# Layer normalisation on ScalarE, five decay buffers, two C-row buffers and a new order of steps

## The chip, the cores and the metric

The kernel runs on one core of a Trainium2 chip. The core has TensorE (PE: matmuls into PSUM banks), VectorE (DVE), ScalarE (ACT), GpSimd (POOL) and SyncE (SP), which here only issues DMA transfers. Each engine works through its own list of instructions in order; semaphores order them against each other. The metric is the device time of one execution in microseconds, lower is better.

## The reference, cut to what matters

Eight batches of 512 tokens with 128 features go one by one through two blocks.

```
xn = layernorm(x)                                  # (x - mean) / sqrt(var + 1e-5)
s  = attention(xn)                                 # own token masked out
g  = silu(sum over 8 experts of gate_e * expert_e(xn))   # top 2 of 8, computed densely
x  = x + s * g
xn = layernorm(x)
s  = mamba(xn)        # rmsnorm, in_proj, conv, selective scan over 512 tokens, out_proj, + xn
g  = silu(routed_expert_ffn(xn))                   # one of 8 experts per token
x  = x + s * g
```

The selective scan keeps, for 256 channels and 16 states, `s = s * dA + dBu` along the tokens, and sums `s * C` over the states.

## The kernel before, in words

**Groups of steps.** The work of a batch is cut into named steps in five groups. A: first layer norm (ln0, xn), transposes xT, gating (gl, gate), attention (q, k, v, s, p, o), dense experts (h0 to h15, m0 to m7, b2), silu. H: second layer norm (ln1, xm), mamba input (hT, xi, z, u, bc, bm, bl), routing (sc, rk, which gives each token its position), dl, ln and du (softplus, delta), put (POOL scatters the tokens to DRAM by position), fetch. S: the scan, with 32 scans i = 2n + h for state n and half of channels h; d is a decay on ACT (exp), b spreads a row of B with a matmul, scan is done by DVE (input times du, then the scan), p multiplies by the row of C on POOL, a adds the product into yacc with an identity matmul (h = 0) and e adds it on POOL (h = 1), c loads a row of C by DMA, spread over the partitions. F: routed expert FFN (w loads expert weights, ld and xs load and transpose tokens, h, y, st stores, get gathers, ft, silu). C: the end of a batch (y, op, xr, out). P: preparation of weights; P.pe (`beta_products`, L926 to L935) is 64 matmuls of one column with 128x128 weights, whose sums are needed by scaled_weights on DVE (dve 2).

**Order.** Five batches overlap: while S and F work on batch b, H is at b+1, A at b+2 and C at b-1 (`AHEAD`, L344). `ROWS` (L59) gives every step a place in a batch, in fractions of a batch, small shifts for ACT, DVE and POOL, and a PSUM bank; `OWN` (L324) gives other places for the first batches. `program` (L364) sorts them into a list for each engine. PE and SP follow the plain order of places. Nothing is decided at run time: an engine that waits holds all that stands behind it.

**The layer norms.** DVE computes mean and variance (`moments`, L1116 to L1122: four bn_stats, four bn_aggr), POOL computes rstd by a power (L1418, L1419; for the second norm also rstd2, L1425 to L1428), and DVE normalises four tiles of 128x128: xn at L1146 and xm at L1214. ACT scales the second by rstd2 (L1001). PE transposes the results (xT L718, x1T L761, hT L765).

**Around the scan.** The decays dA have four buffers (`DECAYS`, L41): decay s waits until scan s - 4 is done (L1083). The rows of C have three (`C_BUFS`, L42): SP may issue the load of row r when all products of row r - 3 are done (L659), and holds its other transfers meanwhile. rk is L786 to L790 on PE, its positions end with L1271 on DVE. gl is L722, q and k L725, v L728, s L736 and L737, p L743, o L752, expert h L823 and m L829, F.h L854, F.y L862 and L864, b L877, a L886 and L888, op L905, dl L800. All work of ACT is issued from L944.

Of the kernel before, what the change touches and what calls it, by code (L numbers as in the profile page):

```python
# [40 lines left out]
DECAYS = 4  # L41
C_BUFS = 3  # L42
# [10 lines left out]
def group_tiles(k):  # L53
# [371 lines left out]
def build(nc, ins, out, xs_dram, ys_dram, kept_dram, c_dram):  # L425
    nc.disable_value_cache = True
    ctx = ExitStack()
    with ctx:
# [151 lines left out]
        def state(s):  # L580

            n, h = divmod(s, NH)
            return st[:, STATES[h][n]]
# [973 lines left out]
```

## Time and profile before

| | us |
|---|---|
| median of 3 runs | 982.8 (982.41 to 982.96) |
| the profiled execution | 983.75 |
| its span | 981.9 |
| PE busy | 855.8 (87%) |
| DVE busy | 810.0 (82%) |
| ACT busy | 608.9 (62%) |
| POOL busy | 587.6 (60%) |
| mean granted clock of PE | 0.936 |

The shares are means over a head of some 150 us in which DVE and POOL have little to do, periods in which all five groups overlap, and a tail in which first A and then H are missing. Timeline rows give the start in us from the start of the span, the length in us, engine, line, operation and count; in brackets stands the idle time before, with what ended it. "busy" is the time in which an engine had something in work; latencies of instructions that follow each other can overlap a little. A granted clock of 1.00 is TensorE's 2.4 GHz, 0.50 is 1.2 GHz.

### The profile page before, as it was taken

Reading aid. Unit: us, or ns where it says so; the run is one execution under the profiler, and the core shown is the slowest. Engines: PE = TensorE matmul, PEld = TensorE weight load, DVE = VectorE, ACT = ScalarE, POOL = GpSimd, SP = SyncE. Lnnn points to the kernel's source line nnn. Section 1 sums busy time; section 2 is a strip of 40 time slices with the busy share of each in tenths; the row PEclk is TensorE's granted clock in tenths of the full one; section 3 lists DMA queues with packets and bytes.
Section 4 is the critical chain, followed back from the end, with each engine's and each line's share of the span. In section 5 each row is a group of like instructions: output and inputs, shape, how many; then the busy total and the mean of one; then the engine's idle time right before and its main releaser. Section 6 shows DMA issues by size and latency. Waiting matters only on the chain.

```text
span 981.9 us, 15767 instructions
## 1 busy us (share of the span) xinstructions
PE 855.8 (87%) x4624; PEld 582.9 (59%) x4624; DVE 810.0 (82%) x1542; ACT 608.9 (62%) x1315; POOL 587.6 (60%) x524
## 2 busy tenths in 40 slices
PE   5997897999699978999799969999799977684995
PEld 3773475766467745766477736776477645452762
DVE  4244537999989889999999998998999989886995
ACT  3424644868467766778477765778477765574661
POOL 0010202848856695848766694848765697669665
PEclk9977699999899999999999998999999989796998
DMA  7200103224323334324323243225322234324542
GB/s 263 88 0 1 44 12 105 72 80 97 115 65 90 96 94 128 76 76 121 94 89 93 75 115 99 76 78 131 100 85 79 77 101 138 98 72 113 156 132 51
DMA packets 79428, 90.27 MB, mean 92 GB/s; under 512 B 8450, under 2 KB 49906, under 8 KB 78834
## 3 DMA queue, kind: packets, MB, share of 16 engines
q1 hardware_dynamic: 77298, 85.07, 29.5%
q0 software_dynamic: 2048, 4.20, 1.5%
q8 instruction: 40, 0.66, 0.3%
q14 instruction: 42, 0.34, 0.1%
HBM read 52.96 MB, written 13.04 MB: 67 GB/s over the span
## 4 chain that ended last, share of the span: by engine, by line
PE 55%; DVE 21%; issue 9%; POOL 8%; ACT 5%; SPq 1%; DMA 1%; DVEq 0%; POOLq 0%
PE work L823 10%; PE work L829 9%; DVE st L1303 7%; PE work L854 5%; PE yacc L888 5%; PE work L864 5%; PE work L752 3%; POOL st L1470 3%; PE work L773 3%; DVE b_row L1296 2%; PE work L796 2%; PE work L743 2%; PE b_row L877 2%; ACT prob L944 1%; PE work L725 1%
## 5 line engine op out<-in xcount | busy, mean ns | idle before, releaser
L1470 POOL TENSOR_TENSOR st<-st,Cs 128x512 f32<-128x512 f32 x249 | 316.8, 1278 | 178.1 <-DVE st L1303 162.9
L944 ACT ACTIVATE dA<-delta,Aneg 128x512 f32<-128x512 f32 x256 | 175.5, 723 | 20.6 <-POOL du L1431 10.7
L888 PE MATMUL yacc<-st,w_ident 128*128 128x512 f32 x256 | 143.6, 650 | 19.5 <-POOL st L1470 19.1
L1303 DVE TENSOR_TENSOR_SCAN st<-dA,dbu 128x512 f32<-128x512 f32 x128 | 154.7, 1209 | 1.4 <-PE yacc L888 0.6
L1303 DVE TENSOR_TENSOR_SCAN st<-dA,b_row 128x512 f32<-128x512 f32 x123 | 148.7, 1209 | 3.1 <-POOL y L1477 3.1
L829 PEld LDWEIGHTS work<-w_w2a,hid 128*128 128x128 f32 x1024 | 124.3, 195 | 29.4 <-issue 13.0
L944 ACT ACTIVATE hsT<-work,hs 128x128 f32<-128x128 f32 x352 | 99.7, 370 | 61.0 <-PE work L854 60.3
L823 PE MATMUL work<-xnT,w_w1a 128*128 128x512 f32 x256 | 134.5, 615 | 0.7 <-ACT dt L944 0.7
L1477 POOL TENSOR_TENSOR y<-y,st 128x512 f32<-128x512 f32 x105 | 133.2, 1269 | 3.0
L829 PE MATMUL work<-w_w2a,hid 128*128 128x128 f32 x1024 | 127.3, 279 | 5.2 <-ACT hid L944 5.2
L944 ACT ACTIVATE hid<-work,w_b1a 128x512 f32<-128x512 f32 x128 | 87.9, 688 | 66.5 <-PE work L823 62.1
L1188 DVE SCALAR_TENSOR_TENSOR acc<-work,gates,acc 128x128 f32<-128x128 f32 x256 | 71.0, 339 | 50.0 <-PE work L829 46.2
L854 PEld LDWEIGHTS work<-xsT,hs 128*128 128x128 f32 x704 | 92.6, 202 | 20.8 <-issue 12.3
L854 PE MATMUL work<-xsT,hs 128*128 128x128 f32 x704 | 98.2, 287 | 1.2 <-ACT hsT L944 1.2
L864 PE MATMUL work<-w_w2f,hsT 128*128 x704 | 98.8, 284 | 0.0
L864 PEld LDWEIGHTS work<-w_w2f,hsT 128*128 128x128 f32 x704 | 86.4, 193 | 20.0 <-issue 17.8
L1296 DVE TENSOR_TENSOR dbu<-b_row,du 128x512 f32<-128x512 f32 x123 | 85.4, 695 | 14.8 <-PE b_row L877 7.3
L1296 DVE TENSOR_TENSOR b_row<-b_row,du 128x512 f32<-128x512 f32 x123 | 84.0, 683 | 2.7
L877 PE MATMUL b_row<-bc,sel_b 96*128 96x512 bf16 x123 | 48.8, 400 | 35.5 <-DVE st L1303 35.5
L888 PEld LDWEIGHTS yacc<-st,w_ident 128*128 128x128 f32 x256 | 46.0, 204 | 56.3 <-POOL st L1470 28.6
L1418 POOL TENSOR_TENSOR ve<-mv,eps 128x4 f32<-128x4 f32 x16 | 3.2, 201 | 113.9 <-DVE mv L1121 113.9
L1440 POOL DMA_INDIRECT xs_dram<-xn_tok,pos x32 | 32.5, 1016 | 51.9 <-DVE pos L1271 43.7
(187 smaller groups left out, 1315.0 us busy)
## 6 DMA issues: line engine op xcount, KB each, us to landing
Cs<-c_dram SPq DMA_DIRECT2D x128, 256.0 KB
hs<-w_w1f SPq DMA_DIRECT2D x88, 258.0 KB, 2.4
xs_in<-xs_dram SPq DMA_DIRECT2D x16, 256.0 KB
ys_dram<-ys SPq DMA_DIRECT2D x16, 256.0 KB, 2.2
w_w1f<-in_w1f_dram SPq DMA_DIRECT2D x1, 2064.0 KB, 7.7
x_in<-in_x_dram SPq DMA_DIRECT2D x8, 256.0 KB
w_w2f<-in_w2f_dram SPq DMA_DIRECT2D x1, 2048.0 KB, 12.8
kept_dram<-x_tok SPq DMA_DIRECT2D x8, 256.0 KB, 2.4
```

The costliest lines, as they stand in the source:

```text
L823: last = mm(w[:], W["w1a"][:, i * 128:(i + 1) * 128], xnT[:], start=True, stop=True)
L829: last = mm(w[:, t * 128:(t + 1) * 128], hid[:, c % 4, t * 128:(t + 1) * 128], W["w2a"][:, c * 128:(c + 1) * 128], start=(c == PER * i), s ...
L854: last = mm(w[:, c * 128:(c + 1) * 128], w1s[:, i % 2, c * 128:(c + 1) * 128], xsT[:, i // 4 % 2, i % 4 * 128:(i % 4 + 1) * 128], start=Tr ...
L864: last = mm(r, hsT[:, i % 2, c * 128:(c + 1) * 128], W["w2f"][:, bass.ds(e * H1 + c * 128, 128)], start=False, stop=(c == HC - 1))
L877: mm(rows_bank(n, b)[:], row_of(n), bc3[:, par], start=True, stop=True).then_inc(sig["B_in"], 1)
L888: mm(yacc[:], ident[:], state(s), start=False, stop=(n == NS - 1)).then_inc(sig["y_sum0"], 1)
L944: return nc.scalar.activation(out, in_, func, **k)
L1188: last = V.scalar_tensor_tensor(acc[:, t], w[:, t * 128:(t + 1) * 128], gates[:, t, i:i + 1], acc[:, t], ALU.mult, ALU.add)
L1296: V.tensor_tensor((dbu0, rows_bank(n, b))[h][:], rows_bank(n, b)[:], du[:, par, h], ALU.mult).then_inc(sig["dBu"], 1)
L1303: V.tensor_tensor_scan(state(s), dA[:, s % DECAYS], (dbu0, rows_bank(n, b))[h][:], 0.0, ALU.mult, ALU.add).then_inc(sig["scan"], 1)
L1470: G.tensor_tensor(state(s), state(s), Cs[:, b.of(NS, n) % C_BUFS], ALU.mult).then_inc(sig["P"], 1)
L1477: G.tensor_tensor(y1[:], y1[:], state(s), ALU.add).then_inc(sig["y_sum1"], 1)
```

## The change

ACT takes over the normalising step of both layer norms. It computes x * rstd + shift with shift = -(mean * rstd), which POOL computes with two more instructions on 128x4 before it signals. `zeros` is a constant for that. ACT waits for rstd, and for the second norm for opx of the batch before (the last reader of the buffer); DVE waits for xn1 of the batch before it overwrites x_tok. The decays get five buffers and their index counts over all batches; the rows of C get two. All places, shifts and banks in ROWS and OWN are new.

```diff
-DECAYS = 4
-C_BUFS = 3
+DECAYS = 5
+C_BUFS = 2
@@ ROWS: 262 rows, all with new places; a few @@
-    ("P", "pe", 0, -1.02692, 2, -3, 0, None),
+    ("P", "pe", 0, -0.58416, 8, -3, -3, None),
-    ("A", "xn", 0, 0.06785, 0, -2, -2, None),
+    ("A", "xn", 0, 0.04088, 0, 0, 2, None),
-    ("S", "c", 15, 0.87337, -1, 6, 3, None),
+    ("S", "c", 15, 1.05620, -2, 4, 0, None),
@@ ACT @@
+                elif name == "xn":
+                    act.wait_ge(sig["rstd0"], b.of(1, 1))
+                    for t in range(NT):
+                        last = go(xn_tok[:, t], x_in[:, par, t], ACT.Identity, scale=rstd[:, t:t + 1], bias=shift[:, t:t + 1])
+                    last.then_inc(sig["xn0"], 1)
                 elif name == "xm":
+                    act.wait_ge(sig["rstd1"], b.of(1, 1))
+                    since(act, sig["opx"], b.of(1, -1))
+                    for t in range(NT):
+                        last = go(xn1_tok[:, par, t], x_tok[:, t], ACT.Identity, scale=rstd1[:, t:t + 1], bias=shift1[:, t:t + 1])
+                    last.then_inc(sig["xn1"], 1)
                     act.wait_ge(sig["xn1"], b.of(1, 1))
@@ decay and scan @@
-                go(dA[:, s % DECAYS], delta[:, par, h], ACT.Exp, scale=Aneg[:, h * NS + n:h * NS + n + 1]
+                go(dA[:, b.of(STEPS, s) % DECAYS], delta[:, par, h], ACT.Exp, scale=Aneg[:, h * NS + n:h * NS + n + 1]
@@ DVE @@
-                elif name == "xn":
-                    dve.wait_ge(sig["rstd0"], b.of(1, 1))
-                    for t in range(NT):
-                        last = V.tensor_scalar(xn_tok[:, t], x_in[:, par, t], mv[:, t, 0:1], rstd[:, t:t + 1],
-                                               ALU.subtract, ALU.mult)
-                    last.then_inc(sig["xn0"], 1)
                     since(dve, sig["kept"], b.of(16))
+                    since(dve, sig["xn1"], b.of(1))
                     V.tensor_tensor(x_tok[:], x_in[:, par], r, ALU.add).then_inc(sig["x1"], 1)
-                elif name == "xm":
-                    dve.wait_ge(sig["rstd1"], b.of(1, 1))
-                    for t in range(NT):
-                        last = V.tensor_scalar(xn1_tok[:, par, t], x_tok[:, t], mv1[:, t, 0:1], rstd1[:, t:t + 1],
-                                               ALU.subtract, ALU.mult)
-                    last.then_inc(sig["xn1"], 1)
@@ POOL @@
-                    last = G.tensor_tensor(rstd_k[:], ve_k[:], neghalf[:], ALU.pow)
+                    lk(g, G.tensor_tensor(rstd_k[:], ve_k[:], neghalf[:], ALU.pow))
+                    lk(g, G.tensor_tensor(ve_k[:], mv_k[:, :, 0], rstd_k[:], ALU.mult))
+                    last = G.tensor_tensor((shift if k == "0" else shift1)[:], zeros[:], ve_k[:], ALU.subtract)
```

What the new tables make of the lists, where the prediction speaks of it (a prime marks the next batch):

```
head, PE,   before: ... A0.m6 A0.m7 P.pe H0.hT ...   H0.dl1 A1.s0 A1.s1 A1.s2 A1.gT A1.s3 A1.h0 A1.p0
            after:  ... A0.m6 A0.m7 H0.hT ...        H0.dl1 P.pe A1.s0 A1.s1 A1.s2 A1.gT A1.s3 A1.h0 A1.p0
period, PE, before: b0 b1 xs0 a15 xs1 h0 h1 a0 xT b2 gl k q op a1 y0 b3 y1 h2 s0 s1 gT s2 s3 v a2 ...
            after:  b0 b1 xs0 a15 xs1 h0 h1 a0 b2 xT y0 gl op k a1 b3 q y1 h2 s0 s1 gT s2 s3 v a2 ...
      ACT,  before: d0 d1 ft d2 d3 F.silu xs0 xs1 h0 h1 xT k d4 gl q y0 ...
            after:  d0 ft d1 d2 d3 d4 F.silu xs0 xs1 h0 xn h1 xT gl k d5 q y0 ...
      DVE,  before: ... bc scan20 bl rk scan21 al m4 scan22 scan23 m5 scan24 ... scan27 du0 scan28 m6 scan29 du1 scan30 m7 scan31 scan0' silu ln0' y'  xn' scan1'
            after:  ... bc scan20 rk scan21 al m4 scan22 bl scan23 scan24 m5 ... scan27 du0 du1 scan28 scan29 m6 m7 scan30 scan31 silu scan0' ln0' y' scan1'
      POOL, before: ... p20 put0 put1 p21 put2 e10 p22 put3 p23 p24 e11 p25 p26 e12 p27 get0-3 du0 e13 p28 p29 du1 p30 e14 p31 ft e15 ln0'
            after:  ... p20 put0 put1 put2 p21 put3 p22 p23 e10 p24 e11 p25 p26 e12 p27 e13 get0-3 du0 du1 p28 p29 p30 e14 p31 ft e15 ln0'
      SP,   before: ... c12 c13 c14 st2 keep c15 fetch xin' w0' ld1' w1' c0' c1' ld2' xr' c2' c3' w2' w3' c4' ...
            after:  ... c12 c13 st2 cw c14 fetch xr' w0' w1' c15 xin' ld1' c0' c1' w2' c2' c3' w3' w4' c4' ...
```

## Rows read from the trace of the kernel before

**Rows 1.** Busy table over five periods, xT to xT; columns after the sum: busy us each

```profile
sum 546.52, PE 498.61 PEld 344.98 DVE 499.98 ACT 377.53 POOL 378.05; mean PE 99.72 PEld 69.00 DVE 100.00 ACT 75.51 POOL 75.61
```

**Rows 2.** The same table for the two halves of one period; PEclk is granted clock

```profile
378.14:442.66 64.52, 63.63 (x383) 45.98 (x381) 60.18 (x111) 45.56 (x105) 39.13 (x35) 1.00 0.27 79
...
442.66:486.84 44.18, 36.37 (x187) 23.25 (x186) 39.95 (x81) 29.90 (x60) 36.79 (x33) 0.92 0.42 117
```

**Rows 3.** Timeline of DVE in that period's second half: start us, length us

```profile
443.99 0.19 DVE L1257 TENSOR_TENSOR more<-work,w_full 128x32 f32<-128x32 f32 x1
...
446.11 0.17 DVE L1271 CAST pos<-posf 128x4 uint32<-128x4 f32 x1
...
484.88 1.42 DVE L1146 TENSOR_SCALAR qkv<-x_in,mv,rstd 128x128 f32<-128x128 f32 x4
```

**Rows 4.** Timeline of POOL in the same half

```profile
447.13 1.08 POOL L1440 DMA_INDIRECT xs_dram<-xn_tok,pos  x1 [2.77 <-DVE pos L1271]
...
480.28 1.26 POOL L1477 TENSOR_TENSOR y<-y,st 128x512 f32<-128x512 f32 x1
...
482.87 0.20 POOL L1418 TENSOR_TENSOR ve<-mv,eps 128x4 f32<-128x4 f32 x1 [1.33 <-DVE mv L1121]
...
483.15 1.05 POOL L1419 TENSOR_TENSOR rstd<-ve,neghalf 128x4 f32<-128x4 f32 x1
```

**Rows 5.** Timeline of PE at the joints of the two halves

```profile
442.66 0.20 PE L786 MATMUL work<-ohb,before_b 128*128 128x8 bf16 x2
...
486.84 0.60 PE L718 MATMUL work<-w_ident,qkv 128*128 128x128 f32 x4
...
488.08 0.39 PE L877 MATMUL b_row<-bc,sel_b 96*128 96x512 bf16 x1 [0.65 <-DVE st L1303]
...
488.31 0.96 PE L722 MATMUL work<-w_gate,xnT 128*128 128x8 f32 x8
...
493.63 1.11 PE L864 MATMUL work<-w_w2f,hsT 128*128 x8
```

**Rows 6.** Costliest groups over the whole run, DVE and ACT (busy, mean ns)

```profile
L1214 DVE TENSOR_SCALAR xn_tok<-x_tok,mv,rstd 128x128 f32<-128x128 f32 x32 | 29.8, 992 | 3.3 <-POOL rstd L1428 3.3
...
L1146 DVE TENSOR_SCALAR qkv<-x_in,mv,rstd 128x128 f32<-128x128 f32 x32 | 11.4, 417 | 4.3 <-POOL rstd L1419 4.3
...
L944 ACT ACTIVATE hx<-xn_tok,rstd 128x128 f32<-128x128 f32 x32 | 10.2, 390 | 15.1 <-DVE xn_tok L1214 15.1
```

**Rows 7.** Head: timeline of PE, and its busy table from 100 to 105 us

```profile
57.08 10.76 PE L933 MATMUL yacc<-w_betaT,w_w1f 128*128 128x1 f32 x64
...
101.97 2.08 PE L736 MATMUL work<-qkv 128*128 128x512 f32 x2
...
115.49 1.50 PE L743 MATMUL work<-w_ident,prob 128*128 128x128 f32 x12 [0.18 <-ACT prob L944]
...
100.00:105.00 5.00, 5.00 (x7) 1.76 (x8) 3.58 (x18) 2.84 (x5) 0.71 (x1) 0.50 0.08 28
```

**Rows 8.** Head: timeline of ACT and PE at the first transposes

```profile
8.91 0.20 ACT L944 ACTIVATE bqs<-w_bq 128x1 f32<-128x1 f32 x1 [6.91 <-DMA w_gate<-in_gate_dram]
...
8.94 1.12 PE L718 MATMUL work<-w_ident,qkv 128*128 128x128 f32 x4 [8.94 <-DMA w_gate<-in_gate_dram]
```

**Rows 9.** C rows: POOL's waits, SP's issues, and POOL's timeline

```profile
POOL st L1470 <- DMA Cs<-c_dram: 14.8, 9, 2.2
...
424.96 1.09 SPq L660 DMA_DIRECT2D Cs<-c_dram  x2
...
428.69 1.27 POOL L1470 TENSOR_TENSOR st<-st,Cs 128x512 f32<-128x512 f32 x1 [1.71 <-DMA Cs<-c_dram]
...
936.33 1.27 POOL L1470 TENSOR_TENSOR st<-st,Cs 128x512 f32<-128x512 f32 x1 [0.50 <-DVE st L1303]
...
938.19 1.27 POOL L1470 TENSOR_TENSOR st<-st,Cs 128x512 f32<-128x512 f32 x1 [0.59 <-DVE st L1303]
```

**Rows 10.** Timeline of DVE in the period of batch 6

```profile
832.43 3.97 DVE L1214 TENSOR_SCALAR xn_tok<-x_tok,mv,rstd 128x128 f32<-128x128 f32 x4
```

More of the change, by code:

```diff
@@ L325 @@
     ("A", 0): (
[4 rows of a table removed]
[4 rows of a table added]
     ),
     ("H", 0): (
-        -1.11900, -1.08467, -1.01476, -0.83547, -0.90068, -0.85797, -0.89443, -0.84069, -0.83471, -0.83140, -0.82978, -0.62226,
-        -0.81859, -0.79895, -0.81765, -0.90515, -0.81371, -0.74442, -0.61163, -0.90703, -0.69090, -0.71827, -0.58703, -0.54773,
-        -0.50916, -0.42023, -1.08490, -1.30874,
+        -1.18130, -1.06491, -1.05613, -1.02584, -1.03955, -0.85206, -0.82195, -0.82119, -0.81775, -0.81765, -0.81158, -0.44602,
+        -0.79856, -0.78129, -0.76470, -0.84007, -0.75073, -0.74593, -0.58004, -0.81765, -0.59953, -0.70707, -0.55657, -0.52952,
+        -0.48284, -0.49093, -0.53779, -0.80928,
     ),
     ("A", 1): (
[4 rows of a table removed]
[4 rows of a table added]
     ),
@@ L496, in build @@
         rstd2 = sb("rstd2", [128, NT])
+        shift, shift1 = sb("shift", [128, NT]), sb("shift1", [128, NT])
+        zeros = sb("zeros", [128, NT])
         xn1_tok = sb("xn1_tok", [128, 2, NT, D])
@@ L1302, in scan @@
                 since(dve, sig["y_sum%d" % h], b.of(NS, user_before(n, h) + 1))
-                V.tensor_tensor_scan(state(s), dA[:, s % DECAYS], (dbu0, rows_bank(n, b))[h][:], 0.0,
+                V.tensor_tensor_scan(state(s), dA[:, b.of(STEPS, s) % DECAYS], (dbu0, rows_bank(n, b))[h][:], 0.0,
                                      ALU.mult, ALU.add).then_inc(sig["scan"], 1)
@@ L1397, in _ @@
             V.memset(eps[:], EPS)
+            V.memset(zeros[:], 0.0)
             V.memset(fe[:], 0.0)
```

536 rows, old and new, of tables (OWN, ROWS, sig) are left out of this document.

## The prediction

> **What bounds the kernel now.** I read the busy table over five equal periods first, then the same table for the two halves of one period, then the timelines of VectorE (DVE), GpSimd (POOL) and TensorE (PE) around the joints of those halves, and last the head and the tail. A period is the time from one batch's transposes of the normalised input (step xT, L718) to the next batch's. Of 109.3 us (546.52 / 5) PE is busy 99.7 and DVE 100.0, ScalarE (ACT) 75.5 and POOL 75.6 [rows 1]. So two engines are near full, but not at the same time. From xT to the rank matmuls (step rk, L786) PE is busy 63.63 of 64.52 us, at full clock: this half is a queue of matmuls and its length is their sum. From rk to the next xT PE is busy only 36.37 of 44.18 us, and DVE 39.95 [rows 2]. In this second half a chain sets the time: DVE finishes the positions at 446.28 (446.11 + 0.17) [rows 3]; POOL starts its scatters at 447.13 and works without a gap of more than 0.3 us until 481.54 (480.28 + 1.26), which is 34.4 us; it then waits 1.33 us for DVE's mean, computes rstd until 484.20, and DVE normalises until 486.30 [rows 3, 4]. xT starts at 486.84, behind the yacc matmuls that need DVE's L1317 and the next p step [rows 5]. POOL, which looks like an engine with a third of its time free, is thus full in the half that counts.
>
> **The normalisations.** Over the run the second one (L1214) takes 32 x 0.992 = 31.7 us of latencies, 29.8 busy; the first (L1146) 11.4: 41.2 us leave DVE, 5.15 per batch [rows 6]. An instruction of L1214 is 2.4 times one of L1146, of the same shape (992 against 417 ns) [rows 6]. L1214 stands among POOL's p steps, and each of which holds POOL for 1.26 to 1.27 us [rows 4, 9]. The Trainium skill (SBUF — State Buffer, "SBUF: two separate sides") says that a two-port DVE instruction and a POOL instruction exclude each other for a whole instruction, which agrees with the 992 ns; by it leaving DVE is worth all of the 31.7 us, by the 417 ns of work alone it would be 13.3. On ACT the nearest row is the scaling of the same tile, 128x128 from SBUF, 390 ns of latency, 10.2 us busy for 32, 1.28 us for four [rows 6]. 64 of them add 20.5 us to ACT, 2.6 per batch, to 75.5 of 109.3: idle time covers it. Were ACT not free when rstd comes, each us of lateness would be one of the chain. The Trainium skill (Perfetto Trace Analysis, "Optimizing Scalar/DVE Operations") warns that a DVE in a 2x mode is faster than ACT; an unhindered L1146 (1.42 / 4 = 0.355 us [rows 3]) agrees, yet four take 1.42 against 1.28 us in line. POOL gains two tiny instructions for each normalisation, about 0.28 us each by the 0.20 us of L1418 and its 0.08 us gap [rows 4]: 0.55 us on the path to rstd.
>
> **What that is worth.** 4.0 of the 5.15 us lie in the first half, where the PE queue is the limit: they only let DVE run ahead. The 1.42 us are in the second half, between y and scan 1. I therefore do not count 5.15 per period but follow the loop through the new order. (a) In the order of PE F.y0 (1.0 us, as L864 x8 with L862) now stands between xT and gl, where PE waited 0.65 us for b2 and for ACT's copy [rows 5]; ACT's copy comes after the four hsT of h1, so gl starts 1.65 instead of 1.47 us after xT, but with y0 done: 0.83 us gained. (b) DVE takes rk before bl instead of behind it (0.69 us, ending right before 443.99 [rows 3]): 0.7 us gained. (c) POOL's list from put0 to e15 holds the same 4 scatters, 4 gathers, 11 p, 6 e, 2 du and ft: 34.4 us stay. (d) DVE enters this half ahead, with scan 27 behind it, so its mean is ready when POOL is: the 1.33 us wait goes. (e) From there to xT: before 486.84 - 482.87 = 3.97 us; now 0.28 + 1.05 + 0.55 for rstd and shift, 1.26 for the next p, 0.05, 0.86 for the yacc matmul and 0.22 for b2, 4.2 us; ACT's normalisation (1.28 after shift) is shorter than that branch. 0.2 us lost. Sum: 0.83 + 0.7 + 1.33 - 0.2 = 2.6 us per period, 6 periods with all stages: **15.6 us**. Bounds: nothing, if (d) fails and ACT is late by the rest; 5.15 x 6 = 31 us, if DVE alone set the time.
>
> In the period of batch 6 (no attention and first experts), DVE is the limit and L1214's 3.97 us lie on its path [rows 10]; with (b) that is 4.5 us, bounds 1 and 6. The last batch has no normalisation: 0.
>
> **The head.** Two things cost there. The first normalisation on ACT stands behind ACT's wait for the small weights: bqs starts at 8.91 and takes 0.20, so the four end at 10.4 and xT goes from 8.94 to 10.5: 1.6 us lost [rows 8]. Worse, the beta products (P.pe, L933: 64 matmuls, 10.76 us, 168 ns each) stood where PE waited for DVE's chain after the first batch's experts [rows 7]; they now stand between dl1 and s0 of batch 1. From dl1's end at 101.97 to the transposes p0 at 115.49 there were 13.5 us, with PE at 1.2 GHz (granted 0.50) [rows 7]. Now: 10.8 for the products, 2 x 2.0 for s0 and s1, 1.1 and 0.6 for s2 and gT if the clock is back, 1.1 for s3, 0.7 for its maximum and 0.8 for the exponential: 19.1, with 0.9 of waits 20.0. So 6.5 us lost, bounds 3 (products and s at the full clock) and 9 (all of it at 1.2 GHz). What they cover no longer, the 10 us after the experts, PE spends idle. Head: **8.1 us lost**.
>
> **The buffers.** In the list of waits no scan waits for a decay, so a fifth buffer for decays gains 0 by itself; it lets ACT issue four decays before the normalisation enters its queue. Two buffers for C rows: the load of row k waits on SP for the products of row k-2 instead of k-3. From issue to use a load takes 3.2 us (second of the pair from 424.96, so 425.5, to 428.69) [rows 9]. In the last batch, where POOL follows DVE's scans, products start every 1.8 us (936.33 and 938.19), so from the end of p(2k-3) to p(2k) there are 4.1 us [rows 9]; where POOL works without gaps, three instructions, 3.75 us. Both cover 3.2 us, by 0.5 to 0.9. What queues behind a waiting load on SP are the expert weights (w), the stores (st) and the fetches of F; ld1 now stands behind c15, which waits for p27, done 12 us earlier. I count 0; without that cover 1.6 us a time (14.8 / 9) [rows 9]. ACT's two new waits (for opx and for rstd) hold decays and hsT behind them; opx is done half a period earlier. DVE's new wait for xn1 before x_tok is overwritten was met long before.
>
> **The sum.** The profiled execution took 983.75 us (span 981.9). 983.75 + 8.1 - 15.6 - 4.5 = 971.7. The median of the runs is 0.95 below the profiled one: **970.8 us**.
>
> **Rivals.** (1) The periods are DVE's: all of the 5.15 us comes back, 31 in six periods. For it: DVE is at 100.0 of 109.3. Against: PE's first half has 0.9 us of slack. 983.75 + 8.1 - 31 - 4.5 - 0.95 = 955. Chance 0.17. (2) Slower: C rows come late. Place: the row loads on SP behind weight loads that wait for ACT; it already happens once per batch with three buffers. Price 1.6 us each, on a POOL that is the chain of the second half; from 12.0 / 7 = 1.7 us per batch on (one new late row) it eats the whole gain, at three per batch it is 1.64 x 3 x 7 = 34 us: 1005. Chance 0.08. (3) The change does not do what it says: the work leaves DVE but the path gets no shorter, because ACT reaches xn late (behind POOL's ft, tanh, two copies and h0) and rstd is 0.55 us later. Then the periods stay, and 983.75 + 8.1 - 4.5 - 0.95 = 986.4. Chance 0.15.
>
> **How the numbers follow.** Forecast (gain of 1.5 to 3.5 us a period, head cost 4 to 10): 0.60, own range 963 to 979. The range must reach rival 1 and rival 3 and leave out only rival 2 and the far ends: 953 to 987. Within 0.2% (981 to 985, about what a measurement can tell from no change) lie the edges of the forecast and of rival 3: 0.05. Slower: rival 2 and most of rival 3, 0.20. Faster: 0.75.
>
> **What would show it.** Periods of about 106.7 us between the L718 groups; POOL unbroken from the first put to e15 with no wait for DVE's mean; DVE waiting in the first half (about 56 of 64 us busy) while PE is full there; DVE's total at 769, ACT's near 630, POOL's near 594 us; L933 between L800 and L736 near 103 us and PE idle for some 10 us from 57; p0 of batch 1 some 8 us later; waits for Cs no more than the 9 of before. Wrong would be: periods at 104 or below (PE's sum is not the limit), waits for Cs in every row, or L933 done in 6 us.

## The result, and the profile after

The changed kernel takes 990.57 us (median of 4 runs, 988.58 to 994.02) against 982.61 for the kernel before: ratio 1.0095, 95% interval 1.0078 to 1.0111. By that ratio it is 0.95% slower, and the medians differ by 8.0 us; the forecast was 970.8 us.

| | before | after |
|---|---|---|
| profiled execution, its span | 983.75, 981.9 | 988.58, 986.7 |
| DVE busy | 810.0 | 774.7 |
| ACT busy | 608.9 | 630.0 |
| POOL busy | 587.6 | 592.5 |
| xT of batch 2 starts at | 159.48 | 174.88 |
| five periods from there, sum and mean | 546.3, 109.3 | 539.7, 107.9 |
| period of batch 6, rk to rk | 97.44 | 94.34 |

In spans: +15.4 until xT of batch 2, -6.6 in five periods, -0.6 in the next first half, -3.1 in the period of batch 6, -0.3 after it; sum +4.8, as 986.7 - 981.9. In the changed kernel xT is L720, rk L788, the scan L1304, all of ACT L946.

The busy table over the five periods, which answers to [rows 1]:

```profile
sum 539.70, PE 499.57 PEld 343.90 DVE 475.67 ACT 390.13 POOL 381.00; mean PE 99.91 PEld 68.78 DVE 95.13 ACT 78.03 POOL 76.20
```

DVE has lost its 4.9 us per period (100.0 to 95.1), and the period only 1.3. The five periods one by one, cut at rk; F.h is the group of 16 matmuls of PE ahead of xT at the end of the second half (before / after, us):

| period | first half | second half | F.h |
|---|---|---|---|
| 1 | 64.30 / 62.30 | 45.64 / 44.22 | 3.62 / 3.27 |
| 2 | 64.51 / 63.91 | 44.19 / 43.53 | 2.01 / 2.02 |
| 3 | 64.54 / 64.35 | 44.18 / 44.20 | 2.01 / 3.24 |
| 4 | 64.53 / 64.49 | 45.70 / 44.28 | 3.62 / 3.65 |
| 5 | 64.51 / 64.14 | 44.18 / 44.28 | 2.01 / 2.98 |
| sum | 322.39 / 319.19 | 223.89 / 220.51 | |

The busy table for the halves of the third period, against [rows 2] (stretch, length, then busy us of PE, PEld, DVE, ACT and POOL with their counts, granted clock, DMA share and GB/s):

```profile
388.84:453.19 64.35, 63.73 (x382) 45.70 (x380) 55.19 (x105) 45.86 (x107) 39.31 (x37) 1.00 0.28 83
453.19:497.39 44.20, 36.55 (x186) 23.62 (x187) 40.72 (x79) 31.66 (x65) 37.62 (x35) 0.92 0.37 107
```

The first half is still PE's sum. This second half, which was to shrink by some 2 us, took 44.18 and takes 44.20. DVE is busy 40.72 of it, where it was 39.95: what left DVE there (xn) came back as bl. POOL's timeline in this half, against [rows 4]:

```profile
457.20 1.09 POOL L1444 DMA_INDIRECT xs_dram<-xn_tok,pos  x1 [2.55 <-DVE pos L1272]
...
471.31 1.26 POOL L1474 TENSOR_TENSOR st<-st,Cs 128x512 f32<-128x512 f32 x1 [0.35 <-DVE st L1304]
...
491.09 1.26 POOL L1481 TENSOR_TENSOR y<-y,st 128x512 f32<-128x512 f32 x1
492.72 0.20 POOL L1420 TENSOR_TENSOR ve<-mv,eps 128x4 f32<-128x4 f32 x1 [0.36 <-DVE mv L1133]
493.00 1.05 POOL L1421 TENSOR_TENSOR rstd<-ve,neghalf 128x4 f32<-128x4 f32 x1
...
494.40 0.20 POOL L1423 TENSOR_TENSOR shift<-zeros,ve 128x4 f32<-128x4 f32 x1
```

From the first put to the end of e15 it takes 35.15 us (34.41 before): POOL now waits for scans in between, and at the end still 0.36 us for the mean. What stands between shift and xT, on ACT and on PE:

```profile
494.46 1.14 ACT L946 ACTIVATE hsT<-work,hs 128x128 f32<-128x128 f32 x4 [1.36 <-PE work L856]
495.47 1.65 ACT L946 ACTIVATE qkv<-x_in,shift,rstd 128x128 f32<-128x128 f32 x4
```

```profile
491.44 1.02 PE L849 MATMUL work<-w_ident,xs_in 128*128 128x128 f32 x4 [2.03 <-DMA xs_in<-xs_dram]
492.37 3.24 PE L856 MATMUL work<-xsT,hs 128*128 128x128 f32 x16
495.45 1.02 PE L888 MATMUL yacc<-u,diagD 128*128 128x512 f32 x2
496.31 1.02 PE L890 MATMUL yacc<-st,w_ident 128*128 128x512 f32 x2
497.17 0.38 PE L879 MATMUL b_row<-bc,sel_b 96*128 96x512 bf16 x1
497.39 0.60 PE L720 MATMUL work<-w_ident,qkv 128*128 128x128 f32 x4
```

ACT takes up xn 0.87 us after shift (494.60), because the copy of the first expert's hsT stands ahead of it; xn ends at 497.12. PE waits for the second load of xs, then runs h0, h1 and the yacc matmuls without a gap, up to xT. The 16 matmuls take 3.24 us here, at a granted clock of 0.60. In the one period of the changed kernel where they ran at 1.00, in 2.02 us, the second half is 43.53 us. The head, against [rows 7], PE and then DVE:

```profile
103.32 13.81 PE L935 MATMUL yacc<-w_betaT,w_w1f 128*128 128x1 f32 x64
117.00 2.05 PE L738 MATMUL work<-qkv 128*128 128x512 f32 x2
...
123.92 2.07 PE L738 MATMUL work<-qkv 128*128 128x512 f32 x2 [2.85 <-DVE delta L1278]
```

```profile
119.20 0.69 DVE L1161 TENSOR_REDUCE nmax<-work 128x1 f32<-128x512 f32 x1 [15.54 <-PE work L739]
121.12 0.69 DVE L1161 TENSOR_REDUCE nmax<-work 128x1 f32<-128x512 f32 x1 [1.23 <-PE work L739]
121.72 0.69 DVE L1276 SCALAR_TENSOR_TENSOR work<-work,ez 128x512 f32<-128x512 f32 x1
...
123.18 0.69 DVE L1278 TENSOR_TENSOR delta<-work,cv 128x512 f32<-128x512 f32 x1
```

The beta products hold PE for 13.68 us. DVE stands idle for 15.54 us meanwhile, although the operands of its next free work (softplus, L1276 to L1278) have been there since 108.4, when ACT ends cv: in its list that work stands behind the maxima of s0 and s1. So s2 waits 2.85 us again, and from s0 to p0 it takes 13.50 us, as before (13.52). The first transposes of p come at 130.50 in place of 115.49.

### The profile page after: what moved, and what is told of

Same layout as the page of the kernel before. It is cut to its first block and busy times, and to the rows that moved or that the text cites. A ratio compares the mean times of both kernels' runs of the same rounds, so it can differ in the third digit from the quotient of the medians.

```text
span 986.7 us, 15806 instructions
## 1 busy us (share of the span) xinstructions
PE 858.6 (87%) x4624; PEld 583.8 (59%) x4624; DVE 774.7 (79%) x1479; ACT 630.0 (64%) x1379; POOL 592.5 (60%) x556
## 5 line engine op out<-in xcount | busy, mean ns | idle before, releaser
L946 ACT ACTIVATE dA<-delta,Aneg 128x512 f32<-128x512 f32 x256 | 175.5, 721 | 7.7 <-POOL du L1435 4.5
L1304 DVE TENSOR_TENSOR_SCAN st<-dA,dbu 128x512 f32<-128x512 f32 x128 | 154.8, 1209 | 2.7 <-ACT dA L946 1.7
L1304 DVE TENSOR_TENSOR_SCAN st<-dA,b_row 128x512 f32<-128x512 f32 x123 | 148.8, 1210 | 6.1 <-POOL y L1481 5.7
L946 ACT ACTIVATE hsT<-work,hs 128x128 f32<-128x128 f32 x352 | 100.0, 369 | 65.8 <-PE work L856 64.9
L831 PEld LDWEIGHTS work<-w_w2a,hid 128*128 128x128 f32 x1024 | 120.3, 192 | 24.1 <-issue 12.2
L825 PE MATMUL work<-xnT,w_w1a 128*128 128x512 f32 x256 | 128.9, 596 | 0.0
L831 PE MATMUL work<-w_w2a,hid 128*128 128x128 f32 x1024 | 124.5, 276 | 0.0
L946 ACT ACTIVATE hid<-work,w_b1a 128x512 f32<-128x512 f32 x128 | 86.4, 686 | 55.8 <-PE work L825 44.5
L856 PE MATMUL work<-xsT,hs 128*128 128x128 f32 x704 | 101.2, 293 | 3.4 <-issue 1.9
L866 PEld LDWEIGHTS work<-w_w2f,hsT 128*128 128x128 f32 x704 | 87.4, 195 | 15.2 <-issue 12.6
```

What stands on the lines that cost most here:

```text
L825: last = mm(w[:], W["w1a"][:, i * 128:(i + 1) * 128], xnT[:], start=True, stop=True)
L831: last = mm(w[:, t * 128:(t + 1) * 128], hid[:, c % 4, t * 128:(t + 1) * 128], W["w2a"][:, c * 128:(c + 1) * 128], start=(c == PER * i), s ...
L856: last = mm(w[:, c * 128:(c + 1) * 128], w1s[:, i % 2, c * 128:(c + 1) * 128], xsT[:, i // 4 % 2, i % 4 * 128:(i % 4 + 1) * 128], start=Tr ...
L866: last = mm(r, hsT[:, i % 2, c * 128:(c + 1) * 128], W["w2f"][:, bass.ds(e * H1 + c * 128, 128)], start=False, stop=(c == HC - 1))
L946: return nc.scalar.activation(out, in_, func, **k)
L1304: V.tensor_tensor_scan(state(s), dA[:, b.of(STEPS, s) % DECAYS], (dbu0, rows_bank(n, b))[h][:], 0.0, ALU.mult, ALU.add).then_inc(sig["scan ...
```

## The experiments

Times are given as ratio to the kernel before, run on the same chip. "Mean period" is a fifth of the time from xT of batch 2 to xT of batch 7 (109.3 before, 107.9 after).

**The beta products.** First (e1) the changed kernel with P.pe moved back:

```diff
-    ("P", "pe", 0, -0.58416, 8, -3, -3, None),
+    ("P", "pe", 0, -1.06000, 8, -3, -3, None),
```

> The changed kernel with one step moved back: the 64 beta products (P.pe) stand again behind the first batch's experts, ahead of H0.hT. Theory H (late, they lie with their whole length on the path: in the changed kernel they run from 103.3 to 117.0, and from s0 to p0 it takes 13.5 us before and after): p0 of batch 1 comes 13 to 14 us earlier, at 117, xT of batch 2 near 161, and the time falls by all of it, from 988.6 to 975. Rival C (the recorded step: DVE's chain covers half of them, the head lost the rest elsewhere): p0 at 123 to 124, time 982.

Measured: 979.37 us, ratio 0.9958 (0.9932 to 0.9983), span 975.8; p0 at 119.49, xT of batch 2 at 163.87, mean period 107.8. That is 11 us of the 13.7. The other 2.7 stand ahead of that stretch: rk of batch 0 comes at 95.04 in place of 92.30. In the later kernels with the products early it comes between 88.2 and 95.0, and the eight executions of this one lie between 971 and 981 us, so one head does not price the edit to a microsecond. By its ratio it makes the changed kernel some 0.4% faster than the one before. The opposite edit (e2), in the kernel before:

```diff
-    ("P", "pe", 0, -1.02692, 2, -3, 0, None),
+    ("P", "pe", 0, -0.60500, 2, -3, 0, None),
```

> The kernel before with only the beta products moved, to between H0.dl1 and A1.s0. Theory H: p0 of batch 1 from 115.5 to about 129, xT of batch 2 from 159.5 to 173, time 983.75 + 13.5 = 997. Rival C (half covered, as recorded: 6.5 us): p0 at 122, time 990.

Measured: 995.93, ratio 1.0137 (1.0120 to 1.0154); p0 at 129.44 (13.95 later), span 994.8 (12.9 longer), periods unchanged (109.1). The rows show the same 13.8 us of products and the same 2.85 us of wait behind them:

```profile
102.31 13.81 PE L933 MATMUL yacc<-w_betaT,w_w1f 128*128 128x1 f32 x64
115.98 2.05 PE L736 MATMUL work<-qkv 128*128 128x512 f32 x2
...
122.91 2.08 PE L736 MATMUL work<-qkv 128*128 128x512 f32 x2 [2.85 <-DVE delta L1277]
```

Theory H holds in kind in both directions (11 and 14 us, where the recorded step had 6.5). The place of this one step outweighs all the rest of the change.

**The normalisations.** In e3 the kernel before, its order and its buffers, has only the two steps moved:

```diff
+                elif name == "xn":
+                    act.wait_ge(sig["rstd0"], b.of(1, 1))
+                    for t in range(NT):
+                        last = go(xn_tok[:, t], x_in[:, par, t], ACT.Identity, scale=rstd[:, t:t + 1], bias=shift[:, t:t + 1])
@@ xm on ACT and shift on POOL as in the change; A.xn 0.06785 to 0.03500 @@
```

> The kernel before, its order, its four and three buffers, with only the two normalisations moved to ACT and shift computed on POOL (xn on ACT between the two hsT of h0 and h1, as in the changed kernel). Theory S (the second half of a period is a ring in which POOL's list, DVE's list and PE's routed experts end within a microsecond of each other, so taking 1.4 us from DVE there leaves the other two; the 4 us in the first half are slack): periods stay within 0.7 us of 108.7 to 110.2, only the period of batch 6 gets 3 us shorter, the first xT comes 1.5 us later; 980 to 983. Rival D (the recorded sum: the 1.33 us wait of POOL for the mean goes, 2.6 us per period with the new order, about 1.1 to 1.4 of it without): periods 107.5 to 108, 974 to 976.

Measured: 984.96, ratio 1.0033 (1.0022 to 1.0045). DVE 38 us less busy (772.0), mean period 109.2, period of batch 6 94.82, first xT at 10.59. Theory S; but the time is a little longer still, by the head and by first halves of 65.0 us. In four of the five second halves POOL no longer waits for the mean at all, as step (d) had it, and they still take 44.5 us. In that order the move is worth nothing where all groups overlap. Now the reverse (e4), the new order with both steps on DVE:

```diff
@@ after: xn and xm on DVE as before, shift gone @@
-    ("A", "xn", 0, 0.04088, 0, 0, 2, None),
+    ("A", "xn", 0, 0.04088, 0, -1, 2, None),
-    ("H", "xm", 0, 0.32013, 2, 2, 2, None),
+    ("H", "xm", 0, 0.32013, 2, 0, 2, None),
```

> The changed kernel, its order and its buffers, with both normalisations back on DVE (xn behind y' and ahead of scan 1', as before) and no shift. Theory S: first xT back at 8.9 (1.5 us gained), periods 0.3 to 1 us longer, the period of batch 6 3 us longer, time 990 to 995. Rival R (the move to ACT is worth the recorded 2.6 per period and the new order of steps costs it again): periods 2 to 3 us longer, time 1003 to 1008.

Measured: 1017.38, ratio 1.0357 (1.0340 to 1.0374), mean period 112.8: more than either theory said, and in the half that both took for PE's. DVE and then PE in a first half:

```profile
540.45 4.67 DVE L1216 TENSOR_SCALAR xn_tok<-x_tok,mv,rstd 128x128 f32<-128x128 f32 x4
...
546.77 1.09 DVE L1190 SCALAR_TENSOR_TENSOR acc<-work,gates,acc 128x128 f32<-128x128 f32 x4
```

```profile
548.06 0.23 PE L864 MATMUL work<-b2p,sel_b 96*128 96x128 bf16 x1 [2.21 <-DVEq L1195]
```

Where I put it, xm stands ahead of m0 and one scan; m0 starts 33.8 us behind xT (31.3 in the changed kernel), and PE waits for the bank that m0 frees. A half that is a queue of matmuls has slack on DVE only between such places. To see which of the two it was, one each (e5, then e6):

```diff
@@ after: xn alone on DVE, POOL computes shift for the second norm only @@
```

> The changed kernel with only the first normalisation (xn) back on DVE, ahead of scan 1'; xm stays on ACT. Theory X (what hurt in the run with both on DVE is xm alone: its 4.67 us stand right ahead of m0, for which PE's y and h wait; xn costs DVE only 1.4 us where POOL and PE end just as late): first xT at 8.9, periods within 0.7 us of 107.5 to 108.7, 986 to 990. Rival Y (every us on DVE counts in the new order, in proportion 1.4 to 5.4 of the 27 us): 995 to 997.

Measured: 991.95, ratio 1.0101 (1.0071 to 1.0131), mean period 108.7, first xT at 8.59. The executions lie between 984 and 999 us, and the median is 2 us above theory X's range; its periods are theory X's: 0.8 us each for xn. If the two add up, 4.1 of e4's 4.9 us are xm's; no run has xm alone on DVE in the new order.

```diff
@@ before: xm alone on ACT @@
```

> The kernel before with only the second normalisation (xm) on ACT; xn stays on DVE, POOL computes shift for the second alone. Theory X (in the order of before xm lies beside a full PE queue, so in the periods it is slack; it shows only in the period of batch 6, where DVE is the limit): first xT at 8.9, periods 108.7 to 110.2 as before, batch 6 3 us shorter, time 980.5. Rival Y (each us off DVE counts): 4 us in each of seven periods, below 960.

Measured: 982.92, ratio 1.0015 (0.9999 to 1.0030), mean period 109.7, period of batch 6 93.77. Theory X in substance, 2 us above its number. DVE lost 26.1 us of busy time (810.0 to 783.9) against the 29.8 of [rows 6].

**The buffers.** Alone in the order of before (e7):

```diff
-DECAYS = 4
-C_BUFS = 3
+DECAYS = 5
+C_BUFS = 2
```

> The kernel before with five buffers for decays and two for C rows, nothing else. Theory N (neither is waited for): 982.5 to 984, and waits for Cs under 20 us. Rival W (C rows come late behind SP's other transfers, 1.6 us each, on a POOL that is the chain of the second half): 990 or more, with waits for Cs in most rows.

Measured: 1018.01, ratio 1.0351 (1.0311 to 1.0391), mean period 113.7. Both theories are wrong in part: it costs 34 us, yet POOL waits for C rows only 11.7 us. The waits of this kernel, of PE and POOL and then of SP's queue (total, times, longest), and the same two of SP's in the kernel before:

```profile
PE work L854 <- DMA hs<-w_w1f: 22.6, 14, 2.7
...
POOL st L1470 <- DMA Cs<-c_dram: 11.7, 9, 1.7
```

```profile
SPq L660 <- POOL st L1470: 441.2, 104, 12.4
...
SPq L640 <- ACT hsT L944: 65.6, 9, 9.5
```

```profile
SPq L640 <- ACT hsT L944: 206.6, 53, 9.5
SPq L660 <- POOL st L1470: 194.1, 60, 5.9
```

SP now stands at the C rows (441 us) and reaches the expert weights (L640) late; PE waits for them at the routed experts (22.6 us, 14 times; no such wait before). And the other way round (e8):

```diff
@@ after @@
-DECAYS = 5
-C_BUFS = 2
+DECAYS = 4
+C_BUFS = 3
```

> The changed kernel with the buffers of before, four for decays and three for C rows, and the new order kept. Theory N: 988 to 991, as the changed kernel, since its waits for Cs are 4.3 us in all. Rival V (the fifth decay buffer is what keeps the scans fed while ACT holds the normalisation): scans wait for decays behind xn, 0.5 to 1.3 us per period, 992 to 998.

Measured: 1019.67, ratio 1.0360 (1.0328 to 1.0393), mean period 113.6. Rival V in kind, six times its size. ACT waits at a decay for the scan that frees its buffer, 52.9 us in all against 2.6, and the experts' relu and the softplus stand behind it:

```profile
590.69 0.72 ACT L946 ACTIVATE dA<-delta,Aneg 128x512 f32<-128x512 f32 x1 [2.66 <-DVE st L1304]
591.44 0.69 ACT L946 ACTIVATE hid<-work,w_b1a 128x512 f32<-128x512 f32 x1
```

So order and buffers belong together: each order loses 29 to 36 us with the other's buffers. Which of the two settings does it was not separated; the waits name the C rows in e7 and the decays in e8.

**Which list sets the second half.** Four edits of the first experiment's kernel ("the base" below, mean period 107.8). First xs early (e9):

```diff
-    ("F", "xs", 0, 0.01212, 1, -2, 1, 1),
+    ("F", "xs", 0, -0.06050, 1, -2, 1, 1),
-    ("F", "silu", 0, 0.99714, 1, 3, -3, None),
+    ("F", "silu", 0, 0.99714, 3, 3, -3, None),
@@ batch 0 keeps 0.01212 @@
```

> Base is the changed kernel with the beta products early (p0 of batch 1 at 119.5, periods 108.6 to 108.7 at their longest, 979.4). Here F.xs0 stands ahead of a14 on PE (a14 waits for POOL's p28 and holds xs0, the load behind it and xs1), and ACT copies xs0 ahead of ft and xs1 ahead of F.silu. Theory J (POOL's list reaches xT by two routes that end within 0.5 us: p28, a14, xs0, load, xs1, h0, a, xT and e15, rstd, xn, xT; this takes away only the first): periods 0.3 to 0.6 us shorter, 975 to 977. Rival K (the route over xs alone sets the period): 1.3 to 2 us shorter, 966 to 970. Rival L (neither; DVE's list does): no change, 979.

Measured: 981.43, ratio 0.9997 (0.9983 to 1.0010), mean period 108.1. Rival L: the wait for xs is gone and nothing comes back. Two joints of this one kernel show what is there instead:

```profile
369.90 1.13 PE L890 MATMUL yacc<-u,diagD 128*128 128x512 f32 x2 [2.25 <-DVE du L1320]
...
372.11 0.60 PE L722 MATMUL work<-w_ident,qkv 128*128 128x128 f32 x4
```

```profile
477.87 1.32 PE L890 MATMUL yacc<-u,diagD 128*128 128x512 f32 x2 [3.36 <-DVE du L1320]
478.99 1.98 PE L892 MATMUL yacc<-st,w_ident 128*128 128x512 f32 x2
...
481.19 1.04 PE L722 MATMUL work<-w_ident,qkv 128*128 128x128 f32 x4
```

PE is earlier and now waits for DVE's C.y. In the first joint it idles 2.25 us and the matmuls up to xT take 2.2 us; in the second it idles 3.36 us and they take 3.3 (granted clock 1.00 over the first stretch, 0.63 over the second). With F.silu left in its place (e9b):

```diff
-    ("F", "xs", 0, 0.01212, 1, -2, 1, 1),
+    ("F", "xs", 0, -0.06050, 1, -2, 1, 1),
```

> As the run before, but ACT keeps F.silu ahead of xs1, so that xs1's copy waits for POOL's ft. Theory J: the routed experts of PE still wait for ft (37.9 to 38.2 us behind rk), periods 0 to 0.3 us shorter than the base, 977 to 979. Rival K: 1.3 us or more shorter.

Measured: 982.21, ratio 1.0002 (0.9991 to 1.0013), mean period 107.9: nothing either. Then bl ahead of rk on DVE (e10):

```diff
-    ("H", "bl", 0, 0.64143, 1, 2, 3, None),
+    ("H", "bl", 0, 0.64143, 1, -1, 3, None),
```

> The base with bl ahead of rk again on DVE (two scans earlier), the rest of the order new. Recorded step (b): pos comes 0.7 us later behind rk and the period is 0.7 us longer in six periods, 983.5. Theory B (bl only changes sides of pos: between pos and DVE's mean stands 0.7 us less, and POOL waits for DVE's mean anyway): pos 0.5 to 0.7 later, mean where it was, periods within 0.2 us, 979 to 980.

Measured: 1031.30, ratio 1.0492 (1.0452 to 1.0532), mean period 115.9. Both numbers were far off, for a reason that neither had: two scans earlier bl meets ACT before its step bm.

```profile
461.36 0.69 DVE L1241 TENSOR_TENSOR bc<-work,bc 32x512 bf16<-32x512 f32 x1 [5.60 <-ACT bc L946]
...
467.07 0.17 DVE L1272 CAST pos<-posf 128x4 uint32<-128x4 f32 x1
```

From rk to pos it takes 9.64 in place of 2.98 us, 6.7 more, and the period is 8.1 us longer; 1.2 of the rest stand between the first put and e15. So a late pos is paid in full. It moves both lists behind it, POOL's and DVE's, so the run doesn't tell them apart. Next the base without shift (e12):

```diff
-go(xn_tok[:, t], x_in[:, par, t], ACT.Identity, scale=rstd[:, t:t + 1], bias=shift[:, t:t + 1])
+go(xn_tok[:, t], x_in[:, par, t], ACT.Identity, scale=rstd[:, t:t + 1], bias=zeros[:, t:t + 1])
@@ the two POOL instructions of shift for the first norm left out @@
```

> The base, leaving out the two POOL instructions that compute shift for the first normalisation, and with zero in its place (the mean isn't subtracted in xn, so the result isn't the reference's). Theory J (ACT takes up xn only when hsT of h0 is done, 0.9 us after shift): 0.55 us less on POOL changes no period by more than 0.2 us, 978 to 980. Rival M (the recorded step (e): rstd's chain over POOL is the end, 0.55 us per period): periods 0.5 us shorter, 976.

Measured: 978.74, ratio 0.9946 (0.9920 to 0.9972), mean period 108.0: theory J. Taken one at a time, the wait for xs and POOL's two instructions of shift are worth nothing. The last three cut DVE's list (e13), POOL's (e15), and both (e14), on the kernel with xs early (mean period 108.1):

```diff
-                    for t in range(NT):
+                    for t in range(NT if i < 6 else 1):
                         last = V.scalar_tensor_tensor(acc[:, t], w[:, t * 128:(t + 1) * 128], gates[:, t, i:i + 1],
```

> Base is the run with xs early (periods 109.0 at their longest, second half 44.5 to 45.0). Left out: three of the four tiles of m6 and of m7 on DVE (so the experts' sum isn't the reference's), 1.65 us of DVE's list between pos and its mean. Theory D (DVE's list from pos to C.y sets the second half: PE waits 3.4 us for du, POOL 0.33 for the mean): 1.6 us less per period, 981.4 - 10 = 971. Theory J' (POOL's list ends 0.33 us behind it, so only that much comes back): periods 0.3 to 0.5 shorter, 978 to 979.

Measured: 975.06, ratio 0.9933 (0.9916 to 0.9950), but mean period 108.0: the 4.5 us that the span is shorter than that of the kernel with xs early are 3.4 of head and 1 of periods and tail. The head is not the cut's: with the same cut in the last run below, xT of batch 2 comes at 162.50, here at 155.31. Theory J'. DVE ran ahead and now waits for POOL's e15:

```profile
689.44 0.76 DVE L1317 SCALAR_TENSOR_TENSOR yacc<-u,w_dskip,y 128x512 f32<-128x512 f32 x1 [0.67 <-POOL y L1483]
```

```diff
-                    G.tensor_tensor(fe[:], fe[:], xn1_tok[:, par], ALU.add).then_inc(sig["r1"], 1)
+                    G.tensor_tensor(fe[:, 0], fe[:, 0], xn1_tok[:, par, 0], ALU.add).then_inc(sig["r1"], 1)
@@ and no shift, as above @@
```

> The same base. Left out on POOL: the two instructions of shift (zero in its place) and three of the four tiles of the ft addition (the result isn't the reference's), 1.45 us of POOL's list between the first put and rstd. Theory D: POOL only waits longer for DVE's mean (0.33 to 1.2 us), periods as the base or 0.5 us less, 979 to 981. Theory P (POOL's list is the chain, as recorded): 1.45 us less per period, 972.

Measured: 979.58, ratio 0.9974 (0.9963 to 0.9985), mean period 108.4. POOL is early and waits; in four of the five joints PE then runs at a granted clock of 0.54 to 0.58 up to xT, so the period is even a little longer:

```profile
699.13 0.20 POOL L1422 TENSOR_TENSOR ve<-mv,eps 128x4 f32<-128x4 f32 x1 [1.18 <-DVE mv L1135]
```

```diff
@@ the cuts of the last two together @@
```

> Both cuts together, 1.65 us on DVE and 1.45 us on POOL. Theory J' (two lists that start at the same pos and end together): only now do the periods fall, by 1.2 to 1.6 us, 971 to 973. Theory D: no more than the DVE cut alone gives. If PE's route over xs were next, the fall would stop at 0.6.

Measured: 965.55, ratio 0.9822 (0.9806 to 0.9838), mean period 105.8, which is 2.2 us less where the two cuts alone gave 0.1 and nothing. Theory J' in kind, with more than its 1.2 to 1.6 us: DVE's list and POOL's start from the same pos, wait for each other at C.y and at rstd, and end together. In the kernel with xs early the clock held up to xT in two of the five periods; their second halves are 43.49 and 43.54 us, and 41.81 and 41.85 with both cuts. That is 1.7 us, the size of the cuts. In the other three PE ran at 0.62 to 0.68 up to xT and they take 44.5 to 45.0; with both cuts the clock was 1.00 in all five and none is above 42.2. The rest of the 2.2 us goes with the clock. In the changed kernel itself PE's way over xs is a third that ends at the same time; taking it away alone (e9) gained nothing.

## Why the prediction was wrong, point by point

The profiled execution is 16.9 us above its forecast of 971.7: 7.3 by the head, 8.4 by the periods, 1.4 by batch 6, less 0.3 in the tail. The median adds 2.9, since it lay 2.0 above the profiled execution and not 0.95 below.

**The head** was forecast at +8.1 and came out at +15.4 (xT of batch 2). The first normalisation behind the small weights was right: 8.94 to 10.42, 1.5 of the 1.6 us. The failed step is the sum 10.8 + s0 + ... = 20.0 for the stretch from dl1 to p0. It took 27.2 (13.7 + 13.5). Of the 7.2 us between, 2.9 are a duration: I took the products at the 168 ns of [rows 7], a mean at a granted clock of 0.65, though the same group showed 0.50 granted at their new place; there they take 214 ns. The rest, 4.3 us, is a cover that does not exist: I let PE's waits of the stretch vanish behind the products, and they moved along, because the DVE work that ends them stands in DVE's list behind the results of s0 and s1. The two runs of the beta products show 11.0 and 13.95 us at p0.

**The periods** were forecast at -2.6 each in six, 15.6 us, and came out at -1.3 each (-6.6 in five). The sixth has only its first half with all stages (-0.6). For the third period, by steps:
- (a) y0 ahead of gl, 0.83 us. The wait of 0.65 us for b2 is gone (0.17 to 0.31 us ahead of y0 now, in two joints), but the first half is only 0.19 us shorter (64.54 to 64.35): PE's sum of this half is the same, and of 0.89 us without work 0.62 are left. Over the five the first halves lost 3.2 us, 2.0 of them in the first.
- (b) rk ahead of bl, 0.7 us. From rk to pos it takes 2.99 in place of 3.45, 0.46 us, and e10 shows that a late pos is paid in full. But bl is not gone, it stands behind pos now, in the very list that (d) needed shorter. That was counted once and cost once.
- (c) "34.4 us stay": 35.15, 0.74 more, with two waits for scans (34.8 in the other four).
- (d) POOL's wait for the mean, 1.33 us. This is the step that failed. The wait did fall, to 0.36, but not because DVE came early: from pos to the mean DVE took 36.3 us before and takes 36.1, and POOL comes 0.74 us later by (c). The words "DVE enters this half ahead" were wrong. DVE is busy 55.19 us of the first half in place of 60.18, and what it saves there ends in waits, the last of them for PE at rk:

```profile
453.73 0.19 DVE L1258 TENSOR_TENSOR more<-work,w_full 128x32 f32<-128x32 f32 x1 [0.50 <-PE work L792]
```

The 1.42 us of xn stood behind the mean and behind C.y and were never on the way to the mean. Nor was this wait a price. In the first and fourth period of the kernel before, POOL does not wait for the mean, and these two are the long ones; in e3 it is the same in four of five. The fourth period of before, and the F.h of the third beside it:

```profile
590.23 0.20 POOL L1418 TENSOR_TENSOR ve<-mv,eps 128x4 f32<-128x4 f32 x1
```

```profile
482.01 2.01 PE L854 MATMUL work<-xsT,hs 128*128 128x128 f32 x16
...
590.23 1.11 PE L847 MATMUL work<-w_ident,xs_in 128*128 128x128 f32 x4 [3.70 <-ACT xsT L944]
591.14 3.62 PE L854 MATMUL work<-xsT,hs 128*128 128x128 f32 x16
```

PE's way over xs ends the half there, with no wait between F.h and xT. I had that way nowhere in the sum.
- (e) 3.97 was to become 4.2 and became 4.67 (492.72 to 497.39), 0.70 more; the other joints show 4.34 to 5.10. ACT's xn takes 1.65 us instead of 1.28, and starts 0.87 late behind hsT; it ends 0.27 us before PE reaches xT by its own work. In the second period, where PE's clock held, the half is 0.65 us shorter than 44.18; in the other four F.h was slow, and it is 44.2 to 44.3.

For the third period that is -0.46 + 0.74 - 0.97 + 0.70 = 0.0 us in the second half, where the forecast had -1.8.

What did make the periods shorter: 3.4 of the 6.6 us lie in the second halves. Two of the five of before held 1.5 us more than their neighbours (45.64 and 45.70 against 44.18), where F.h ran 3.62 us at a granted clock of 0.50 instead of 2.01 at 1.00, behind 3.70 us of idle time instead of 1.60. I took the mean of the five and did not look at why they differ. In the new order F.h starts 38.8 to 39.2 us behind rk in place of 39.4 to 39.8, so a slow F.h comes less dear, but it comes in four of five. The other 3.2 us lie in the first halves, and no run tells why 2.0 of them are in the first.

**Batch 6** was -4.5 and is -3.1; e3 and e6, which move only normalisations, give -2.6 and -3.7. So L1214's share (3.97) was right in kind and too large, and (b)'s share did not come on top.

**The buffers** were counted at 0, and within the new order nothing waits more: POOL's waits for C rows fell to 4.3 us (6 times, longest 1.1), against 14.8 in [rows 9]. What I wrote of them was still too light. "A fifth buffer gains 0 by itself" holds for the order of before, where ACT waited 8.1 us for decays' buffers; in the new order the old settings lose 29 us, with 52.9 us of such waits.

**The rivals.** Rival (3), the work leaves DVE but the path gets no shorter, at 986.4, was the right one, with chance 0.15, and it named ACT's lateness rightly; its head was 7 us too cheap. Its main reason is another: joined lists, and PE's way over xs beside them. Rival (1) had the DVE at 100.0 of 109.3 for it, which is what misled: DVE was near full and still not what the period waited for. Rival (2) didn't come, but e7 shows its place: SP behind C rows, paid at the expert weights rather than at POOL. DVE's total (774.7 for 769), ACT's (630.0) and POOL's (592.5) came out near what was said, and so did the place of the products near 103 us and the 12.6 idle us from 58.

The Trainium skill (SBUF — State Buffer, "SBUF: two separate sides") made L1214's 992 ns an exclusion by POOL. The same instruction takes 1116 ns in e4, with 4.67 us for four next to POOL's products, and 26.1 us leave DVE's busy time when it goes to ACT; the rule agrees. The trace of before has it at both, too: with no work on POOL the four of batch 0 take 1.11 us, against 3.97 in [rows 10], where three of the four take 1.30 us each, as long as one of POOL's products.

```profile
66.17 1.11 DVE L1214 TENSOR_SCALAR xn_tok<-x_tok,mv,rstd 128x128 f32<-128x128 f32 x4 [3.33 <-POOL rstd L1428]
```

The rule says what DVE gets back, not whether the path does.

## What to carry to other kernels

A stretch in which each of two engines waits for the other at the end is priced by cutting both lists. The 5 us that left DVE moved the periods of the old order by nothing (109.2 for 109.3), and cutting DVE or POOL alone by some 1.5 us moved them by 0.1 or nothing, both together by 2.2. When a block of matmuls moves to a place with idle time, ask what ends that idle time and whether it stands in the other engine's list behind the results that the block delays; if so, the block costs all of its length, at the clock of the new place. When periods that do the same work differ in length, look at why before taking their mean: here two of five already showed the way over xs and the lower clock. And an engine's waits hold only for the order in which they were measured: the new order waits 4.3 us for C rows and 2.6 for decays' buffers with five and two, and loses 29 us with four and three.

## What the hardware showed beyond that

The granted clock of TensorE fell at times right beside the path, behind idle time of PE. In one kernel the matmuls from C.y to xT took 2.2 us after 2.25 us idle (clock 1.00) and 3.3 after 3.36 (0.63). The length of the last wait does not decide it alone: with POOL's list cut, waits of 1.90 and 2.02 us there were followed by 0.54, with both lists cut one of 2.38 by 1.00; F.h before it had run at 0.77 to 0.78 in the first two and at 1.00 in the third. In the head the same order ran with a granted clock of 0.59, 0.59 and 0.78 in one execution and 0.68, 0.74 and 0.91 in another, whose xT of batch 2 came 5 us earlier. Each row: 20 us of the head, of the kernel with the beta products early and of the one with xs early:

```profile
70.00:90.00 20.00, 13.54 (x37) 8.04 (x38) 7.54 (x12) 8.82 (x19) 0.20 (x1) 0.59 0.00 1
90.00:110.00 20.00, 17.21 (x41) 6.62 (x40) 8.55 (x36) 10.85 (x18) 3.17 (x3) 0.59 0.04 11
110.00:130.00 20.00, 16.96 (x82) 10.53 (x82) 10.70 (x25) 11.87 (x22) 3.56 (x3) 0.78 0.10 31
```

```profile
70.00:90.00 20.00, 15.03 (x42) 7.23 (x43) 8.57 (x18) 8.57 (x18) 0.00 (x0) 0.68 0.00 1
90.00:110.00 20.00, 11.86 (x40) 4.94 (x38) 12.29 (x40) 14.01 (x23) 5.20 (x5) 0.74 0.04 12
110.00:130.00 20.00, 19.68 (x107) 13.49 (x105) 6.95 (x21) 9.52 (x18) 1.51 (x2) 0.91 0.10 30
```

That is why kernels whose totals differ by a few us are compared here by their periods. And a scale and a bias that are both tiles make ACT's instruction longer: xn takes 490 ns on 128x128, where the copy with a scale alone takes 390.
